# A subject's weight table and a ring of sample buffers: the table moved to the head of the load queue, the ring from 8 slots to 16

## The reference

```
x: (128, 128, 1024) float32; itok_B_0_7: (128,) int32; weights: (8, 128, 128) float32
w = weights[subjects]                       # (128, 128, 128)
out = x + einsum('bct,bcd->bdt', x, w)
```

## Time and profile before

| | |
|---|---|
| median of 3 runs | 335.07 us (334.43 to 335.13) |
| the profiled execution: span from the first to the last instruction | 330.9 us |
| around that span, against the median | 4.2 us |
| mean granted TensorE clock | 0.988 |
| TensorE busy | 234.2 us, 71% |
| VectorE busy | 156.8 us, 47% |
| GpSimd busy | 37.8 us, 11% |
| DMA | 134.78 MB, mean 407 GB/s |

### The profile page before, as it was taken

The page is one execution under the profiler, slowest core; times in us unless marked ns, Lnnn a source line. Parts: engine busy times, 40 slices in busy tenths (PEclk is TensorE's granted clock), DMA queues, the critical chain, the costliest instruction groups (busy, mean ns, idle before and its releaser), DMA issues.

```text
span 330.9 us, 2706 instructions
## 1 busy us (share of the span) xinstructions
PE 234.2 (71%) x512; PEld 93.6 (28%) x512; DVE 156.8 (47%) x128; POOL 37.8 (11%) x133
## 2 busy tenths in 40 slices
PE   0069999976876866866866866866867767767750
PEld 0024444332332332322322322322322322322310
DVE  0017777745445445445445445445445445445450
POOL 0011111101111111111111111111111111111000
PEclk9999999999999999999999999999999999999995
DMA  7996999999999999999999999999999999999997
GB/s 272 391 409 245 364 420 419 419 421 423 420 420 420 420 421 421 421 422 420 420 420 420 421 422 422 420 420 420 419 421 421 423 421 420 420 420 421 421 421 308
DMA packets 35893, 134.78 MB, mean 407 GB/s; under 512 B 2097, under 2 KB 3122, under 8 KB 35890
## 3 DMA queue, kind: packets, MB, share of 16 engines
q10 hardware_dynamic: 18466, 67.64, 50.3%
q1 hardware_dynamic: 17424, 67.11, 50.0%
HBM read 67.63 MB, written 67.11 MB: 407 GB/s over the span
## 4 chain that ended last, share of the span: by engine, by line
DMA 75%; PE 17%; DVE 3%; issue 1%; ACTq 0%; POOLq 0%; SPq 0%; POOL 0%
DMA out<-ring 46%; DMA ring<-x 24%; PE products L126 17%; DMA table<-weights 5%; DVE ring L142 3%; POOLq L97 0%; ACTq L151 0%; ACTq L168 0%; SPq L82 0%; ACTq L167 0%; POOLq L102 0%; POOLq L92 0%; POOL selected L102 0%
## 5 line engine op out<-in xcount | busy, mean ns | idle before, releaser
L126 PE MATMUL products<-ring,selected 128*128 128x512 f32 x512 | 234.2, 604 | 84.6 <-DMA ring<-x 65.1
L142 DVE TENSOR_TENSOR ring<-products,ring 128x1024 f32<-128x1024 f32 x128 | 156.8, 1225 | 163.2 <-PE products L126 163.2
L126 PEld LDWEIGHTS products<-ring,selected 128*128 128x128 f32 x512 | 93.6, 191 | 224.3 <-issue 162.5
L102 POOL COPY selected<-table 128x128 f32 x128 | 37.6, 294 | 272.7 <-PE products L126 253.0
L185 POOL MEMSET const-float32-0.0<- 128x1 f32 x1 | 0.1, 98 | 0.1
L185 POOL MEMSET const-bfloat16-1.0<- 128x1 bf16 x1 | 0.1, 101 | 0.0
L185 POOL MEMSET const-uint8-127<- 128x1 uint8 x1 | 0.1, 101 | 0.0
L185 POOL MEMSET const-float32-1.0<- 128x1 f32 x1 | 0.1, 98 | 0.0
L185 POOL BASE_LOAD x1 | 0.0, 17 | 0.2 <-issue 0.2
## 6 DMA issues: line engine op xcount, KB each, us to landing
ring<-x SPq DMA_DIRECT2D x63, 1024.0 KB, 11.4
out<-ring ACTq DMA_DIRECT2D x63, 1024.0 KB, 22.9
ring<-x SPq DMA_DIRECT2D x2, 512.0 KB, 10.7
out<-ring ACTq DMA_DIRECT2D x2, 512.0 KB, 10.3
table<-weights ACTq DMA_DIRECT2D x1, 512.0 KB, 16.7
subject_row<-subjects ACTq DMA_DIRECT2D x1, 0.5 KB
```

What stands on the lines that cost most here:

```text
L102: nc.gpsimd.tensor_copy(selected[:, k, :], table[:, bass.ds(subject * mixed, mixed)]).then_inc(weights_selected, 1)
L126: product = nc.tensor.matmul(products[:, k, cols], selected[:, k, :], ring[:, s, g, cols], start=True, stop=True)
L142: nc.vector.tensor_tensor(ring[:, s, g, :], products[:, k, :], ring[:, s, g, :], ALU.add).then_inc(sum_ready[k], 1)
```

## The change

The load of the table goes from ScalarE's queue, where it was the second transfer, to SyncE's queue, where it is the first, ahead of all loads of x. The ring has 16 slots in place of 8, so that there are 4 turns of 32 samples in place of 8 turns of 16; the ring takes 128 KB of each partition in place of 64 KB. The size of a transfer, the number of transfers and the work of the engines for each sample are the same.

```
-SLOTS = 8
+SLOTS = 16
...
         def _(sp):
...
+            sp.dma_start(table[:].rearrange("c (n d) -> c n d", n=n_subjects),
+                         weights.rearrange("n c d -> c n d")).then_inc(table_loaded, DMA)
             go_round(0, first=True)
...
         @block.scalar
         def _(act):
             act.dma_start(subject_row[:], subjects.rearrange("(a b) -> a b", a=1)).then_inc(subjects_loaded, DMA)
-            act.dma_start(table[:].rearrange("c (n d) -> c n d", n=n_subjects),
-                          weights.rearrange("n c d -> c n d")).then_inc(table_loaded, DMA)
```

## The result

The changed kernel takes 328.75 us (median of four runs, 328.55 to 329.07) against 334.75 us for the one before (four runs, 334.38 to 335.13): a ratio of 0.9832 with a 95% interval of 0.9807 to 0.9856. The forecast was 331.0 us with a range of 329.8 to 333.2.

What follows compares the result with a forecast made beforehand. DMA bandwidth, about 421 GB/s for 134.78 MB, was taken as the bound. Terms -3.06 - 0.77 - 0.2 = -4.0 us took the span from 330.9 to 326.9 us; plus 4.2 us gave 331.0 us, range 329.8 to 333.2.

Steps and rivals of the forecast that it cites:

- the hole: DMA engines idle between 24 and 32 us, no load in flight between 25 and 30 us; 3.06 us lost.
- -3.06 us for the idle time: Term for 24 to 32 us: neither queue runs dry any more, so all 3.06 us of idle go.
- the small pieces at the head: The table's 512-byte pieces alone at the load queue's start: taken as 0 more, at most some 2 us more.
- the tail covered: End of the run: 10.7 us of stores remain, the last sample needs 4.8 us, so the tail stays.
- SyncE's issues held: Load queue: issues are held until older loads are carried, replacing SyncE's waits for stores, 261.5 us in total.
- either part alone enough: Early table or 16 slots alone would do most of removing the 3.06 us of idle at 24 to 32 us.
- the step from span to time: Adds 4.2 us of launch and end, taken as untouched, to the profiled span of 326.9 us, giving 331.0 us.
- the slow stretch: From 32 to 38 us engines count as busy at 313 GB/s; half of the 1.54 us, 0.77 us, was forecast won.
- the lead of the loads: Groups by which loads run ahead of stores: forecast 4.3, before about 5; a store then takes about 17 us.
- Nothing gained: Rival: what is saved at 25 us is given back at the end; 334.5 to 335.5 us, chance 0.06.
- Slower: Rival: stores beside a full load queue run at 313 GB/s for 58 us; 345 us, chance 0.06.
- Held issues of SyncE that hold ScalarE's back: Variant of the rival "Nothing gained": SyncE's held issue also delays ScalarE's stores; 334.5 to 335.5 us.

Runs made afterwards that it cites:

- slots_only: 16 slots in place of 8 against the kernel before, table still second in ScalarE's queue; 329.23 us, ratio 0.9849 to the kernel before.
- table_only: 8 slots in place of 16 against the changed kernel, table still at the head of the load queue; 328.55 us, ratio 0.9838 to the kernel before.
- pause3: Against table_only (early table, 8 slots): in the last turn SyncE's first load also waits for the store of slot 3; 328.79 us.

## Why the prediction was off

**Right.** The bound, and where the time was lost: the hole opens because the first store waits for the late table while eight slots are carried. The single terms held too: first matmul forecast at 7.4 us (7.57), first store at 14.0 us (14.96), released by x and not by the table; -3.06 us for the idle time (3.04); next to no cost of the small pieces at the head (0.25 us by their own row, and 0 to 24 us together cost 3.45 us against 3.74 before); the tail covered, if 0.4 us longer; SyncE's issues held, its waits for stores gone; either part alone enough. The span was forecast at 326.9 us and is 326.8 us.

**Wrong, the step from span to time.** "The median of the runs, 335.07 us, is 4.2 us above the span (launch and end, which the change doesn't touch)." Two things were hidden in the 4.2 us. The kernel before lies 2.45 us above its span; the other 1.7 us were the distance from the profiled execution to the median one, and the profiled one had a shorter hole and no late engines at its end. So the cure was worth more in the median execution than in the one that I read. And the 2.45 us are not untouched: the change to rounds of 16 groups takes 0.67 us off. In medians the 6.0 us are 5.35 us of span (332.3 to 326.95) and 0.67 us around it. Of the 5.35 us, the pair of profiled executions shows 4.1 us, and the other 1.25 us are that distance.

**Wrong, a size.** "I take half, 0.77 us" for the slow stretch: all 1.54 us went. Every kernel here with a hole has such a stretch behind it, and slots_only, as late but without a hole, has none. That the span still came out at 326.8 us, with 0.77 us more gained here and 0.2 us more in 4 to 24 us, is owed to small losses: 0.1 us more at the start, 0.4 us more at the tail, and what is left in the rounding of 421 GB/s over 282 us, where one unit in the last place of 421 is 0.7 us. So the exact hit on the span is partly luck. With the full 1.54 us the forecast of the time would have been 330.3 us, still 1.5 us above what was measured; so it is the step from span to time that failed.

**Wrong, the lead of the loads.** A store was forecast at 17 us and takes 22.6 us. By 100 us the loads had moved 23.47 - 0.52 MB and the stores 17.09 MB, so the lead is 5.6 groups and not 4.3, and the prediction's own (lead - 1) x 4.98 then gives 22.9 us. The step that failed is "14.0 + 0.9 = 14.9 us" for the stores' first bytes. The 0.9 us were read from a store alone on the engines; behind a full load queue the first bytes came between 18.5 and 19 us. It changes nothing in the sum.

**The rivals.** "Nothing gained" at the tail: the loads' lead stayed above what the last sample needs. "Slower" by a full load queue beside the stores: 282 us of just that ran at 421 GB/s. Held issues of SyncE that hold ScalarE's back: not seen in 63 issues.

What stayed open: why packets slow down where the queues are short; what in the round of 16 groups shortens the time around the span; and why some executions end with late engines. Those make up 1.0 us of the 1.3 us between the two profiled spans of the kernel before, but whether they also make its spread (spans over 2.1 us, against 1.0 us for table_only) isn't shown.

## What to carry to other kernels

In a kernel bound by its transfers, look for the first moment at which the load queue is empty and ask what frees its next slot: here a 0.5 MB table, interleaved with the loads, moved the first store by 11 us, and with 8 slots each microsecond of delay from 24.6 us on cost one microsecond at the end. A small input that all the work needs goes to the head of the queue, and then a ring only has to be deep enough to keep both queues filled; 8 slots do what 16 do, 4 cost 16% more than 8. Before a forecast is made from one profiled execution, ask how its own time stands to the median, since a stall that varies is worth its median and not the one that was read.

## What the runs showed of the hardware

- A queue of loads that is full holds its issuer for 4.5 us in the median and up to 11.3 us, and the other issuer's DMAs still take 378 ns each to issue.
- Behind a full load queue the first bytes of a store come some 3.4 to 4 us after its issue (changed kernel, issued at 14.96 us, first bytes between 18.5 and 19 us; slots_only, 26.14 us and between 29.5 and 30 us); beside an empty one it was 0.9 us.
- DMA engines can count as busy and move a third less: 281 GB/s at a share of 1.02 behind a hole, against 421 GB/s at 1.03 with filled queues. With four slots it was 358 GB/s at 0.96. The share of busy time doesn't show it, the bandwidth does.
- The Trainium skill (DMA: Bandwidth & Descriptors, Issuing engines are not separate DMA queues) says that DMAs of different issuers interleave on the same engines. The runs agree: the table took 16.66 us to land beside a filled load queue, and 4.2 us ahead of it.
- In pause3 TensorE had nothing to do from 276 to 285.6 us. Its granted clock was at full speed (2.4 GHz) from 276 to 278 us, 0.63 in the mean of the next 2 us, at half (1.2 GHz) from 280 to 288 us, and at full again from 290 us on.
- 512-byte packets alone moved 344 GB/s (3 to 4 us of the changed kernel).
